# Cross attention on one core: new orders for the first pairs, an earlier residual load, and a last sample mixed by halves of its heads

## What is computed

```python
mu, var = mean(x, (1, 2)), var(x, (1, 2))
xn = (x - mu) * rsqrt(var + 1e-5) * gamma + beta
q  = Wq @ xn + bq                   # 8 heads x 64 channels, 256 positions
kv = Wkv @ context + bkv            # 8 heads of keys, 8 of values
att = softmax(q^T k / sqrt(64))     # 256 x 256 per head
y   = att v                         # per head, then the heads stacked
out = x + Wo @ y + bo
```

## Time and profile before

| what | value |
|---|---|
| median of 3 executions | 728.36 us (728.31 to 729.72) |
| the profiled execution, whole | 729.8 us |
| its span, first to last instruction | 728.0 us |
| mean granted TensorE clock | 0.986 of full |
| busy: TensorE, VectorE, ScalarE, GpSimd | 92%, 93%, 85%, 78% |
| DMA moved | 47.68 MB, 65 GB/s |

### The profile page before, as it was taken

How to read it: one execution, slowest core, us unless ns; L and a number is a source line. 1 busy time by engine, 2 the same in 40 slices (tenths; PEclk the granted TensorE clock), 3 DMA queues, 4 the chain that set the end, 5 groups by cost and what they waited for, 6 DMA issues and landing times.

```text
span 728.0 us, 29894 instructions
## 1 busy us (share of the span) xinstructions
PE 671.5 (92%) x11268; PEld 448.2 (62%) x11268; DVE 676.2 (93%) x1124; ACT 620.7 (85%) x2248; POOL 566.8 (78%) x360
## 2 busy tenths in 40 slices
PE   7995999999999999999999999999999999989986
PEld 6763666566666656666665666665666666656654
DVE  1895999999999999999999999999999999999993
ACT  2885888899888889988889988889998888988883
POOL 2784688788888878888887888888788888778863
PEclk7997999999999999999999999999999999999999
DMA  5202222222222222222222222222222222222110
GB/s 123 52 26 75 71 55 67 75 74 72 74 59 61 68 70 70 70 70 65 58 68 70 70 72 65 63 62 70 70 70 75 58 59 70 73 73 59 47 46 23
DMA packets 74823, 47.68 MB, mean 65 GB/s; under 512 B 33748, under 2 KB 74708, under 8 KB 74772
## 3 DMA queue, kind: packets, MB, share of 16 engines
q1 hardware_dynamic: 72450, 46.46, 23.9%
q10 hardware_dynamic: 2322, 0.53, 0.4%
HBM read 25.96 MB, written 4.19 MB: 41 GB/s over the span
## 4 chain that ended last, share of the span: by engine, by line
PE 59%; DVE 19%; issue 8%; SPq 8%; ACT 3%; DMA 1%; POOLq 0%; POOL 0%; ACTq 0%; DVEq 0%
PE z L466 29%; PE fill L432 24%; DVE neg_max L621 9%; DVE probs_t L634 7%; SPq L346 6%; PE z L477 3%; ACT probs L561 3%; PE z L491 1%; DVE y L677 1%; DVE spread L665 1%; SPq L298 1%; DMA x_res<-in_x 1%; SPq L309 1%; DMA bq_col<-in_L_xattn_bq 1%; DVE recip L627 1%
## 5 line engine op out<-in xcount | busy, mean ns | idle before, releaser
L722 POOL TENSOR_TENSOR probs<-probs,recip 128x1024 f32<-128x1024 f32 x256 | 482.4, 1895 | 132.3 <-DVE recip L627 131.4
L561 ACT ACTIVATE probs<-fill,neg_max 128x256 f32<-128x256 f32 x1024 | 473.6, 488 | 80.1 <-DVE neg_max L621 77.2
L621 DVE TENSOR_REDUCE neg_max<-fill 128x4 f32<-128x1024 f32 x256 | 307.5, 1202 | 16.9 <-PE fill L432 15.5
L634 DVE STREAM_TRANSPOSE probs_t<-probs 128x1024 f32<-128x1024 f32 x256 | 310.6, 1222 | 2.9 <-POOL probs L722 0.9
L432 PE MATMUL fill<-c,t 64*128 64x256 f32 x2048 | 285.9, 400 | 28.6 <-ACT probs L561 25.4
L432 PEld LDWEIGHTS fill<-c,t 64*128 64x128 f32 x2048 | 185.0, 187 | 117.3 <-ACT probs L561 84.9
L466 PE MATMUL z<-probs_t,ctx_keys 32*64 32x256 f32 x8192 | 254.5, 381 | 1.8 <-DVE y L677 1.3
L561 ACT ACTIVATION_READ_ACCUMULATOR probs<-fill,neg_max 128x1 f32 x1024 | 225.0, 220 | 0.0
L466 PEld LDWEIGHTS z<-probs_t,ctx_keys 32*64 32x64 f32 x8192 | 174.9, 131 | 67.7 <-issue 35.4
L570 ACT ACTIVATE t<-z,d_col 128x512 f32<-128x512 f32 x128 | 88.4, 741 | 5.4 <-PE z L444 5.4
L577 ACT COPY z_sb<-z 128x1024 f32<-128x1024 f32 x64 | 62.0, 1034 | 7.3 <-PE z L466 7.3
(11 more groups left out here) (42 smaller groups left out, 132.0 us busy)
## 6 DMA issues: line engine op xcount, KB each, us to landing
ctx_keys<-ctx_turned SPq DMA_DIRECT2D x512, 32.0 KB, 1.9
x<-in_x SPq DMA_DIRECT2D x64, 128.0 KB, 2.8
c<-in_ctx SPq DMA_DIRECT2D x64, 128.0 KB, 2.7
ctx_rows<-in_ctx SPq DMA_DIRECT2D x128, 32.0 KB, 1.8
x_res<-in_x SPq DMA_DIRECT2D x32, 128.0 KB, 2.3
out<-y SPq DMA_DIRECT2D x32, 128.0 KB, 1.8
wq<-in_L_xattn_Wq ACTq DMA_DIRECT2D x2, 128.0 KB
wv<-in_L_xattn_Wkv SPq DMA_DIRECT2D x2, 128.0 KB
```

Source lines behind the costliest of these rows:

```text
L561: ins = act.activation(probs[:, k % SLOTS, g, :], bank[:, K * qt:K * qt + K], ACT.Exp, bias=neg_max[:, k, g:g + 1], accum_out=denom[:, k, ...
L621: dve.tensor_reduce(neg_max[:, k, :], fill[k % PAIRS_OF_BANKS][:, :, :].rearrange("p o (t k) -> p (o t) k", t=QT), AX.X, ALU.max, negate=T ...
L634: dve.transpose(probs_t[p][:, s, :, :, hp, :, :].rearrange("p b o t j -> p o t b j"), probs[:, k % SLOTS, :, :].rearrange("p (o t) (b j) - ...
L722: pool.tensor_tensor(p, p, recip[:, k, :].unsqueeze(2).broadcast_to([128, 2 * QT, K]), ALU.mult).then_inc(probs_ready, 1)
```

## The change

Seven edits:

1. New order tables for pairs 0, 1 and 2 on TensorE, ScalarE, VectorE and GpSimd.
2. `residual` of pairs 0 and 1 moves from 24.35 to 1.50 in SyncE's table.
3. The warm-up has three parts: 13 matmuls as before, 4 after the first `mean` matmul and 1 after the first `var` matmul.
4. A table for pair 30: its `project_out` goes from 30.26 to 29.50 and its `result` from 32.35 to 30.20; the rest of that table is `STEADY`.
5. The second sample of pair 31 is mixed by halves of its heads: twice 64 matmuls of 128 columns in place of 64 of 256. The first half waits for 6 turns, the second for 8.
6. The last `divide` (step 7 of pair 31) runs on VectorE, between the last two turns.
7. The second piece of the last `z` copy runs on VectorE (`copy_last_z`), beside the first on ScalarE.

```diff
-WARM_UP = 12
+WARM_UP = (13, 4, 1)
@@ PE_ORDERS, pair 0
-    0: (at('scores', -1.006, -0.588, 2.530, 3.339, 5.430, 9.769, 10.701, 12.533)
+    0: (at('scores', -0.012, 0.642, 2.532, 3.295, 4.091, 8.757, 9.273, 11.429)
...
+    30: (at('scores', 0.000, 1.200, 3.500, 5.030, 7.250, 10.150, 10.920, 13.570)
+         + at('mix', 18.050, 18.820, 20.270, 21.800, 22.560, 24.010, 24.770, 25.460) + at('project_out', 29.500)
...
@@ SYNC_ORDERS
+    0: (at('load_x', -8.74) + at('load_c', 14.57) + at('load_ct', 2.69) + at('spread_context', 2.49)
+        + at('residual', 1.50) + at('store', 32.85)),
+    1: (at('load_x', -8.74) + at('load_c', 14.57) + at('load_ct', 2.69) + at('spread_context', 2.49)
+        + at('residual', 1.50) + at('store', 32.85)),
...
@@ mix
-                elif i == MIXES:
+                elif i == MIXES and not pair.last():
                     wait(pe, turned, pair.count(STEPS, STEPS))
+                elif pair.last() and i >= MIXES:
+
+                    half, first = (i - MIXES) // 2, (i - MIXES) % 2 == 0
+                    if first:
+                        wait(pe, turned, pair.count(STEPS, STEPS - HP // 2 * (1 - half)))
+                    n = S // 2
+                    for b in range(KB // 2 * (1 - first), KB // 2 * (2 - first)):
+                        for g in range(2):
+                            for a in range(QB):
+                                r = 32 * a
+                                mm = pe.matmul(z[64 * g:64 * g + 64, a, S * s + n * half:S * s + n * half + n],
+                                               ctx_keys[p][r:r + 32, b, s, :],
+                                               probs_t[p][r:r + 32, s, b, g, HP // 2 * half:HP // 2 * (half + 1), :, :],
+                                               start=(b == 0), stop=(b == KB - 1))
...
+            def copy_last_z():
+
+                pair = Pair(0, NPAIR - 1)
+                wait(dve, mixed, pair.count(PS, PS))
+                wait(dve, summed_out, pair.shift(-1).count(1, 1))
+                dve.tensor_copy(z_sb[:, :, :, :].rearrange("p s h (t a j) -> p a (s h t) j", t=QT, a=QB)[:, 2:4, :, :],
+                                z[:, 2:4, :].rearrange("p a (g j) -> p a g j", j=32)).then_inc(z_ready, 1)
+
+            def divide_last():
+
+                pair, k = Pair(0, NPAIR - 1), STEPS - 1
+                wait(dve, recip_ready, pair.count(STEPS, STEPS))
+                p = probs[:, k % SLOTS, :, :]
+                dve.tensor_tensor(p, p, recip[:, k, :].unsqueeze(2).broadcast_to([128, 2 * QT, K]), ALU.mult
+                                  ).then_inc(probs_ready, 1)
```

More of the change, by code:

```diff
@@ L80 @@
         + at('mean_var', -25.790) + at('spread', -15.340) + at('sample_var', -14.190)
-        + at('turn_context', 2.526) + at('result', 31.226) + at('weights', 11.853)),
-    1: (at('max', -1.008, 2.743, 4.034, 6.049, 7.710, 11.782, 11.984, 13.353)
-        + at('recip', 3.530, 4.051, 6.075, 10.094, 11.941, 12.904, 15.055, 17.964)
-        + at('turn', 7.060, 10.754, 10.757, 12.181, 13.239, 14.072, 19.603, 21.755) + at('moments', -25.592)
-        + at('mean_var', -24.385) + at('spread', -12.499) + at('sample_var', -10.944)
-        + at('turn_context', 7.927) + at('result', 32.649)),
@@ L87 @@
-    2: (at('max', 1.059, 2.979, 5.350, 6.188, 7.303, 10.937, 10.937, 15.144)
-        + at('recip', 4.680, 6.001, 6.989, 7.578, 9.734, 13.272, 16.941, 18.028)
-        + at('turn', 7.269, 8.328, 9.019, 11.086, 14.321, 15.637, 19.402, 20.745) + at('moments', -27.595)
-        + at('mean_var', -26.976) + at('spread', -17.375) + at('sample_var', -13.886)
-        + at('turn_context', 1.977) + at('result', 31.715)),
+        + at('turn_context', 8.082) + at('result', 31.730) + at('weights', 12.626)),
@@ new lines @@
+    1: (at('max', -1.895, 0.735, 3.188, 7.375, 8.465, 13.482, 13.684, 14.947)
+        + at('recip', 3.548, 3.551, 8.231, 10.134, 13.141, 14.496, 16.161, 17.867)
+        + at('turn', 8.425, 8.478, 10.991, 14.200, 14.630, 15.084, 20.774, 21.814) + at('moments', -25.953)
+        + at('mean_var', -25.450) + at('spread', -11.093) + at('sample_var', -10.282)
+        + at('turn_context', 8.266) + at('result', 32.666)),
+    2: (at('max', 1.208, 3.588, 5.693, 6.121, 6.757, 8.989, 9.109, 13.290)
+        + at('recip', 5.629, 5.737, 6.335, 6.776, 8.973, 11.593, 16.664, 18.935)
+        + at('turn', 6.524, 8.953, 8.972, 9.055, 11.912, 13.547, 19.594, 20.649) + at('moments', -27.060)
+        + at('mean_var', -23.429) + at('spread', -18.095) + at('sample_var', -16.961)
+        + at('turn_context', 4.324) + at('result', 32.680)),
@@ L92 @@
+    30: (at('max', 0.970, 2.250, 4.510, 6.440, 8.230, 11.130, 12.830, 14.590)
+         + at('recip', 4.450, 6.380, 8.140, 9.070, 10.850, 13.670, 15.430, 18.190)
+         + at('turn', 7.280, 9.130, 9.990, 11.970, 13.730, 15.490, 19.590, 21.350) + at('moments', -28.920)
+         + at('mean_var', -25.790) + at('spread', -15.340) + at('sample_var', -14.190)
+         + at('turn_context', 1.890) + at('result', 30.200)),
 }
@@ L125, in first, with last @@
         return isinstance(self.j, int) and self.c == 0
+    def last(self):
+        return isinstance(self.j, int) and self.c == NPAIR - 1
     def parity(self):
@@ L364, in _, with warm_up @@
         def _(pe):
-            def warm_up():
-                for _ in range(WARM_UP):
+            def warm_up(i):
+                for _ in range(WARM_UP[i]):
                     pe.matmul(fill[1][:, 1, 0:128], ones[:, :], ones[:, :], start=True, stop=True)
@@ L592, in steps @@
                             output_value_steps()
-                    else:
+                    elif not (owner.last() and item == 1):
                         copy_z(owner, item)
@@ L688, in steps @@
                     elif kind == "turn":
+                        if owner.last() and item == STEPS - 1:
+                            divide_last()
                         turn(owner, item)
@@ L705, in steps @@
                     elif kind == "result":
+                        if owner.last():
+                            copy_last_z()
                         result(owner)
@@ L749, in steps @@
                     if kind == "divide":
-                        divide(owner, item)
+                        if not (owner.last() and item == STEPS - 1):
+                            divide(owner, item)
                     elif kind == "root":
```

58 lines of the change are left out of this document (34 added, 24 removed).

## The result

| | before | changed |
|---|---|---|
| median of the runs (us) | 728.47 (726.37 to 729.81, 8 runs) | 723.22 (722.26 to 726.45, 8 runs) |
| ratio to before | | 0.9932, 95% interval 0.9916 to 0.9948 |
| the profiled execution, and its span | 729.8, 728.0 | 723.0, 721.2 |

What follows compares the result with a forecast made beforehand. It took the middle as dense (VectorE 93%, TensorE 92% busy), with gains only in the first slices and the end: 9.3 + 1.9 = 11.2 us off the 728.36 median gives 717.2 us, range 715.8 to 721.2.

Steps and rivals of the forecast that it cites:

- head, up to K (93.29): Start of program to issue of pair 3's context keys: forecast at 84.0 instead of 93.29, a gain of 9.3 us.
- middle, K to T: From pair 3's context keys to turn 4 of pair 31: both kernels run the same order, no gain.
- end, from T: Turn 4 of pair 31 to end of span: halved mixing, VectorE division and side-by-side copies gain 1.9 us.
- Clock at the start: Added warm-up matmuls hold TensorE's full clock through weight products and first projection; 3.3 us reach the first exponentials.
- the rival at 719.1: Clock falls at 11 to 12 us, the first projection runs at half clock, 1.9 us lost; chance 0.15.
- Hole ahead of result 0: VectorE's 7.49 us idle before pair 0's result vanishes with `x_res` loaded early; result reached at 57.5 without wait.
- The new waits: VectorE waits for x before `moments` of pair 3 (1.1 us) and of pair 4 (2.3 us).
- From there one steady period less 1.84: Pair 2's context keys to pair 3's: a steady 21.44 us less the maximum and moments now ahead, 19.6 us.
- The halves' rate: Rival: in the last mixing, records not columns set the pace, a half lasts 3.7 us; 719.5, chance 0.08.
- sign of being wrong, over 3 us: At the end, a half of the last mixing taking over 3 us, against 2.1 forecast, would show the prediction wrong.
- more is late in the new orders: Rival: further in-order waits, followed only on VectorE and SyncE, cost gain; 720 to 724 us, chance 0.13.
- the load is not what ends the hole: Rival: the 7.5 us idle before pair 0's result stays, only 5.2 us gained; 723.2, chance 0.03.

Runs made afterwards that it cites:

- the early loads with small products: Changed kernel with x of pairs 3 and 4 loaded ahead of the context keys, plus seven unread small matmuls in TensorE's stops at the end; 716.27 us.
- the old end: Changed kernel with edits 4 to 7 undone, 724.16 us; the same end with x of pairs 3 and 4 loaded early, 718.46 us.

## Why the prediction was wrong

What failed in short: the sum asked whether TensorE's clock holds at the start alone, and had no term for its fall behind the second new wait (1.2 us) and in the last projection (1.3). It also had the second half of the mixing too short (by 1.15, with a stop of 0.63 that it did not know) and the way of x behind the context keys (by 0.5 and 0.6, in two passes).

Against the profiled execution of before the forecast was 729.8 - 11.2 = 718.6; measured 723.0. The 4.4 us between them, by the prediction's own steps:

| step | forecast | measured |
|---|---|---|
| head, up to K (93.29) | 84.0, gain 9.3 | 86.47, gain 6.8 |
| middle, K to T | 0 | gain 0.6 |
| end, from T | gain 1.9 | loss 0.6 |
| sum | 11.2 | 6.8 |

- **Clock at the start: half right.** "I take it that it holds" is right up to 12 us and wrong for the projection. This is near the rival at 719.1. Full clock up to the projection gives the 0.86, the projection gives 0.9 of its 1.9; the first row maximum came 2.9 earlier and not 3.3 to 3.6, and 0.76 of the 2.9 is that the products started at 7.89 and not at 8.65. In 9 of 11 profiles with the new warm-up the clock fell between 10 and 14 us, so "holds" was not the likely case.
- **Hole ahead of result 0: right.** No wait, at 57.99, forecast 57.5.
- **The new waits: right in place, short in size.** Forecast 1.1 and 2.3; measured 1.45 and 2.92. The way from `turn_context` to the landing of x, 16.2 in the forecast, took 16.7 and 16.8 in the two passes. So `turn_context` of pair 1 ended 0.6 late, x of pair 4 landed at 63.3 and not at 62.1, and `ctx_keys` of pair 2 went out 1.3 late.
- **From there one steady period less 1.84: right where the clock holds, and the clock had no term.** "To that of pair 3 goes one steady period ... 19.6": measured 20.76 (65.71 to 86.47). TensorE ran dry behind the wait for 2.77, its clock fell, the scores took 2.08 and the mixing behind them 2.48 instead of about 2, and VectorE waited again (0.91 at 73.04). Where the clock held behind a wait of 3.46 or 3.69, the stretch took 19.32. The sign was in the trace of before: "at half again behind the hole" stands in the prediction's first part, and no term carries it.
- **The end: the second half and the projection.** "Turn 7 ... 0.67 later than before" is right: from turn 4 to the last turn 7.19, before 6.51. The division on VectorE took 1.18 (forecast 1.2), and the copies until the projection 1.28 against 1.98 (gain 0.7, as forecast). The second half was to end 2.05 after its turn; it took 3.2 (4.46 less the turn's 1.25), so the halves gave 0.65 and not 1.8. And a term that the sum did not have: the projection at half clock, 1.31. In sum -0.68 + 0.65 + 0.70 - 1.31 = -0.6.
- **The halves' rate: the mechanism right, the length not.** The parts of a half took 1.38 and 1.11, 2.5 together, where 3.7 would have meant that columns buy nothing: this rival is out. The 2.1 were too low by the stop and by 0.4: with its stop of 0.63 the second half lasts 3.12. The prediction's sign of being wrong, over 3 us, came, but not by the rate that it was meant for.
- **Profile and median.** The forecast of the median missed by 6.0, that of the profile by 4.4: the changed kernel's profiled execution was at its median, before's 1.4 above. In before's trace 1.0 of the 1.4 is one period in the middle, from the result of pair 26 to that of pair 27, that took 22.4 and not 21.4; the other 0.4 wasn't found. The sum had no term from the middle, so as far as this period goes it was right to take the same 11.2 from the median. But the 0.6 that the table has for the middle comes from it, and head and end by themselves missed by 5.0.

The rival "more is late in the new orders" (720 to 724) is the one that held the time, with 0.13, but by luck: no further wait for data was late in the new orders, and what was missing is the clock, the way of x and the halves. The rival "the load is not what ends the hole" names 723.2 itself, and that is luck too, as the hole is gone. The range was too narrow on the upper side, as the clock was asked only about the start.

What stays open: what the stop inside the halves is. Its place moves with the number of instructions ahead of it. Instruction packets of 16 KB pass in these microseconds, but not in the stops themselves, so the fetch of instructions is only a guess. Why the clock falls in one execution and not in the next, with the same work in the same places, no run here shows. The Trainium skill (TensorE: Matmul & The Clock Gate, Part 1: The HAM clock gate) says that TensorE's activity is watched over a window that runs freely, so that the same kernel differs from run to run. The spread of the profiles agrees, and proves no more than that.

## What to carry to other kernels

When a wait goes, write down what the queue behind it delivers next and at what time, and move those loads in the same edit; here moving the residual's loads gave 2 to 4 us, and moving two loads of x with their waits gave another 7.8, some 6 of it in the head. Price a new wait on the busiest engine with what TensorE does meanwhile: where it ran dry the stretch behind ran partly at half clock in three of six profiles, for 1.4 to 2.9 us, so that belongs into the range. And before two profiles are set side by side, find out in which period each stands off its own median.

## What was not expected of the hardware

- TensorE's clock fell from 1.00 to 0.50 at 12 to 13 us with the engine busy for 2.84 of the 3 us from 8 and 1.78 of the 2 from 11; in the profile of the early loads with small products the same busy times (2.84 and 1.78) kept 1.00. Of the eleven profiles with the new warm-up nine have the fall. So with a busier TensorE the fall came later, and it was not ruled out.
- At the end the clock fell in four of the eight profiles with the changed end and no products in the stops (three times within the last projection), and in neither of the two with them, which is too few to tell. It also fell near the end in two of the four profiles with the old end, where no half is.
- Behind the second wait the clock held after TensorE had been idle for 3.31 and 3.54 us, and fell after 2.77, 3.33 and 3.65. The length of the idle time did not decide it.
- Matmuls of 128 columns on eight tiles ran 128 records in 2.5 us, 20 ns each. The Trainium skill (TensorE: Matmul & The Clock Gate, "Wait — 56ns, not 53.3ns?") has starts never closer than about 25 ns; here the trace does not agree, for records on different tiles.
- In a stream of such short matmuls TensorE stopped for 0.20 to 0.91 us at a fixed record (75, or 71 with four records more ahead of it, or 87 with twelve fewer). With matmuls of 256 columns in the same place, 128 records took 3.71 with no stop in the timeline.
